# Softmax rows transposed on TensorE: probabilities, identity and output bank typed float32r instead of float32

## What is computed

```python
q, k, v = jnp.einsum('bsx,xMnd->Mbnsd', x, qkv)              # 16 heads of 64
a = jnp.einsum('bnsd,bntd->bnst', q, k) * q.shape[-1] ** (-0.5)
cum = jnp.cumsum(rpe_bias[:, :s], axis=-1)
rel = jnp.arange(s)[:, None] - jnp.arange(s)[None, :]
bias = jnp.where(rel >= 0, cum[:, jnp.clip(rel, 0)], PAD)    # PAD = -30000: causal
a = jax.nn.softmax(a + bias, axis=-1)
mix = jnp.einsum('bnst,bntd->bnsd', a, v)
attn = jnp.einsum('bnsd,ndx->bsx', mix, out_w)
x = layernorm(x + attn)
x = layernorm(x + ffn(x))    # ffn: sigmoid(xr W_r) * (relu(xk W_k)^2 W_v), xr and xk mixed with the token before
```

## Time and profile before

| | |
|---|---|
| median of 3 runs | 1161.54 us (1153.31 to 1162.71) |
| the profiled execution, its own time | 1157.7 us |
| its span, first to last instruction | 1156.0 us |
| PE busy | 1106.1 us, 96% |
| PE weight loads busy | 791.9 us, 69% |
| DVE busy | 809.3 us, 70% |
| ACT busy | 731.1 us, 63% |
| POOL busy | 6.4 us, 1% |
| DMA, share of 16 engines on the queue of SP | 62.1% |
| granted TensorE clock, mean | 0.99 of full speed |

### The profile page before, as it was taken

How to read it: one execution, slowest core, us unless ns; L and a number is a source line. 1 busy time by engine, 2 the same in 40 slices (tenths; PEclk the granted TensorE clock), 3 DMA queues, 4 the chain that set the end, 5 groups by cost and what they waited for, 6 DMA issues and landing times.

```text
span 1156.0 us, 21563 instructions
## 1 busy us (share of the span) xinstructions
PE 1106.1 (96%) x6973; PEld 791.9 (69%) x6973; DVE 809.3 (70%) x2121; ACT 731.1 (63%) x1857; POOL 6.4 (1%) x15
## 2 busy tenths in 40 slices
PE   6899999999999999999999999999999999999994
PEld 3666666766677777676777676777666777767773
DVE  2666666666657777776778777778776778777756
ACT  3666667665656676675766676767666667667633
POOL 1000000000000000000000000000000000000000
PEclk9999999999999999999999999999999999999998
DMA  8856565675657666656577656676756666665710
GB/s 200 222 142 150 140 153 145 152 186 137 155 135 168 160 166 161 169 144 174 134 176 171 166 149 155 163 177 164 185 135 155 164 169 158 169 164 144 234 40 20
DMA packets 113005, 180.71 MB, mean 156 GB/s; under 512 B 13152, under 2 KB 69360, under 8 KB 112896
## 3 DMA queue, kind: packets, MB, share of 16 engines
q1 hardware_dynamic: 110736, 178.42, 62.1%
q10 hardware_dynamic: 2160, 0.92, 0.3%
HBM read 58.41 MB, written 20.22 MB: 68 GB/s over the span
## 4 chain that ended last, share of the span: by engine, by line
PE 84%; DVE 5%; DMA 4%; issue 3%; ACT 2%; SPq 2%; POOL 0%; DVEq 0%; ACTq 0%
PE ps_o L1018 22%; PE ps_rows L977 21%; PE ps_t L994 17%; PE ps_m L952 9%; PE ps_m L957 5%; PE ps_m L1034 4%; PE ps_o L994 3%; DMA stacks<-k_lo 2%; DVE pt L684 2%; PE ps_rows L1090 1%; SPq L300 1%; DVE prob L660 1%; DMA prob<-in_L_attn_x 1%; ACT pt L519 1%; DVE mix_sb L691 1%
## 5 line engine op out<-in xcount | busy, mean ns | idle before, releaser
L501 ACT ACTIVATE prob<-prob,low 128x128 f32<-128x128 f32 (+7 forms) x512 | 394.5, 772 | 111.9 <-DVE low L660 106.0
L660 DVE CUSTOM_DVE_ANT_0 prob<-ps_rows,table 128x128 f32<-128x128 f32 (+7 forms) x512 | 379.9, 750 | 52.8 <-PE ps_rows L977 33.9
L977 PE MATMUL ps_rows<-stacks 128*128 128x512 f32 (+3 forms) x1536 | 401.1, 372 | 10.7 <-DMA stacks<-k_lo 6.1
L994 PE MATMUL ps_t<-ident,prob 128*128 128x128 f32 x1984 | 311.4, 278 | 6.4 <-ACT pt L519 3.5
L994 PEld LDWEIGHTS ps_t<-ident,prob 128*128 128x128 f32 x1984 | 231.4, 141 | 90.3 <-issue 74.6
L1018 PE MATMUL ps_o<-pt,v_pair 128*64 128x512 f32 (+3 forms) x1536 | 270.1, 494 | 0.0
L977 PEld LDWEIGHTS ps_rows<-stacks 128*128 128x128 f32 x1536 | 246.1, 190 | 32.0 <-DMA stacks<-k_lo 7.0
L684 DVE COPY pt<-ps_t 128x256 f32<-128x256 f32 (+2 forms) x320 | 178.2, 565 | 124.8 <-PE ps_t L994 124.2
L1018 PEld LDWEIGHTS ps_o<-pt,v_pair 128*64 128x64 f32 x1536 | 102.2, 137 | 177.5 <-issue 165.2
L519 ACT ACTIVATE pt<-ps_t 128x512 f32<-128x512 f32 (+3 forms) x352 | 162.8, 463 | 95.9 <-PE ps_t L994 95.6
L952 PE MATMUL ps_m<-x_cur,w_cur 128*128 128x512 f32 x250 | 131.6, 608 | 5.2 <-DVE q_lo L646 2.0
(11 more groups left out here) (118 smaller groups left out, 607.2 us busy)
## 6 DMA issues: line engine op xcount, KB each, us to landing
stacks<-k_hi SPq DMA_DIRECT2D x126, 256.0 KB, 4.6
stacks<-k_lo SPq DMA_DIRECT2D x126, 256.0 KB, 5.1
inv_all<-inverse_sums SPq DMA_DIRECT2D x128, 128.0 KB, 3.3
stacks<-q_hi SPq DMA_DIRECT2D x63, 256.0 KB, 4.0
stacks<-q_lo SPq DMA_DIRECT2D x63, 256.0 KB, 4.3
mix_transposed<-mix_sb SPq DMA_DIRECT2D x62, 256.0 KB, 3.8
table<-bias_by_distance SPq DMA_DIRECT2D x64, 192.0 KB, 3.6
mix_tile<-mix_transposed SPq DMA_DIRECT2D x24, 512.0 KB, 4.7
```

Source lines behind the costliest of these rows:

```text
L501: nc.scalar.activation(row, row, ACT.Exp, bias=low[:, r:r + 1], scale=-1.0, accum_out=total[:, r:r + 1]).then_inc(s_exp, 1)
L660: nc.vector.tensor_tensor_reduce(prob[:, r % PSLOTS, 0:width], ps_rows[:, score_at(r):score_at(r) + width], table[n % 2][:, h, 0:width][:, ...
L977: ins = nc.tensor.matmul(ps_rows[:, at + c0:at + c1], q_st(h, n)[:, P * i:P * i + P], k_st(h, n, low_part)[:, c0:c1], start=(low_part == 0 ...
L994: ins = nc.tensor.transpose(t_bank[TBANK[k]][:, P * b:P * b + P], prob[:, r % PSLOTS, at:at + P], ident[:, :])
```

## The change

The tiles `prob` and `ident` get a second name with type fp32r, and the 2304 transposes of probabilities (L994) read and write by the new types: data `prob_r`, identity `ident_r`, and the bank viewed as fp32r. `prob_r` lies on the same bytes as `prob` (it is allocated first and given back, and `prob` takes its place); DVE and ACT still write `prob` as f32, and the evacuations still read the banks as f32. `ident_r` is a tile of its own: POOL copies `ident` into it once, and PE waits for that copy ahead of its first instruction. The other transposes (`inv`, `x1`, x, the weights) stay f32. No other instruction changes, nor does the order of PE, DVE, ACT or SP.

```diff
+        with nc.sbuf_tensor("prob_r", [P, PSLOTS, SEQ], F32R) as prob_r:
+            pass
+        prob = sb("prob", [P, PSLOTS, SEQ])
         ident = sb("ident", [P, P])
+        ident_r = sb("ident_r", [P, P], F32R)
...
-        prob = sb("prob", [P, PSLOTS, SEQ])
...
+        s_identr = sem("identr")
...
             pool.affine_select(out=ident[:, :], in_=ident[:, :], compare_op=ALU.not_equal, fill=1.0, base=0,
                                pattern=[[-1, P]], channel_multiplier=1).then_inc(s_const, 1)
+            pool.wait_ge(s_const, 2)
+            nc.gpsimd.tensor_copy(ident_r[:, :], ident[:, :]).then_inc(s_identr, 1)
...
         def _(pe):
             pe.wait_ge(s_const, 2)
+            pe.wait_ge(s_identr, 1)
...
-                        ins = nc.tensor.transpose(t_bank[TBANK[k]][:, P * b:P * b + P], prob[:, r % PSLOTS, at:at + P],
-                                                  ident[:, :])
+                        ins = nc.tensor.transpose(t_bank[TBANK[k]][:, P * b:P * b + P].bitcast(F32R),
+                                                  prob_r[:, r % PSLOTS, at:at + P], ident_r[:, :])
```

## The result

The changed kernel takes 1129.81 us (median of 4 runs, 1128.80 to 1134.16) against 1158.34 (4 runs, 1153.31 to 1162.71): ratio 0.9766, 95% interval 0.974 to 0.9791. The forecast was 1100 us, 58 less than before. The profiled execution took 1129.46 us, and its span is 1127.7, 28.3 less than the 1156.0 before.

What follows compares the result with a forecast made beforehand. PE's own instructions were taken to set the pace; 1.82 us saved in each of 32 steps, 58 us off 1157.7, gave 1099.5, predicted as 1100. Likeliest range 1068 to 1115 (0.53); 1068 to 1164 holds 0.83.

Steps and rivals of the forecast that it cites:

- What bounds the kernel: One step's chain: PE's own instructions set the pace, PE leaving it only once, about a microsecond, for DVE to empty `ps_o`.
- The copy on POOL: Start of the kernel: POOL's copy of `ident` and PE's wait for it cost 0; without cover 0.6 us at most.
- The saving per transpose: Transposes of probabilities on PE: 75 ns each in fp32r against 109 in f32, saving 34 ns.
- rival of no change: An fp32r transpose still costs about 109 ns through weight load or double streaming; 1158 to 1162 us; load mean 190; chance 0.17.
- How much reaches the step: A step's 72 transposes: 0.8 us from 42 beside DVE's closed work, 1.02 from the other 30, 1.82 in all.
- DVE's block: Stretch 719.98 to 734.30 of a step, 42 transposes: DVE's work is closed from a bias to the copy of `ps_o`.
- The cap: Where DVE is nearly full, faster PE can only close DVE's gaps of 0.76 us; 0.8 counted in place of 1.43.
- The sum: Whole kernel: 1157.7 less 58 us (32 x 1.82) gives 1099.5; predicted 1100.
- What is late next: Next step's first score waits for head 0's `k_lo`; its DMA lands 1.2 us early and stays covered.
- Slower: With 128 columns an fp32r instruction falls back to 222 ns, 113 ns more per transpose; about 1418 us; chance 0.11.
- Large gain: A transpose at 56 ns: 1081 us with DVE's limit in force, 1036 without; chance 0.06 for under 1068.
- Small gain: Transposes shorten, but PE also meets ACT's evacuations in the 734.3 to 738.2 stretch; about 1131 us, 1115 to 1150; chance 0.13.

Runs made afterwards that it cites:

- The tail: The changed kernel with sequences of f32 and fp32r transposes and products added behind PE's last work; alone, an f32 transpose took 109 ns, an fp32r one 85 ns.

## Why the prediction was wrong, point by point

**What bounds the kernel: mostly right.** PE's own instructions set the pace in the rest of the step, and what they saved there arrived whole (0.58 to 0.60 us). But I took the one place where the chain leaves PE for PE's only wait, and that was wrong. The chain hides short waits, because a run's time in it holds what PE waited inside the run.

**The copy on POOL: right.** Cost 0, ratio 1.0005.

**The saving per transpose: wrong in size.** I took 34 ns for each of 72. Measured: 109 - 85 = 24 ns, and nothing for the first of each run, of which a step has 16. That is 56 x 24 ns = 1.34 us a step in place of 2.45, or 19 ns a transpose. The step that failed is the choice of 75 ns on the argument that the transpose's own load is the short one. The tail shows the f32 load in 62 ns (with 64 rows) and the fp32r one in 85. The line through the fp32r products (64 ns) was no lower bound either, since it knows only the stream. The Trainium skill's sustained 81 ns for a weight load and matmul pair of 128 columns ("TensorE: Matmul & The Clock Gate", on the back-to-back issue gap) was nearer than my 75: this case shows 85. (By the 81 ns my sum would have been 52.5 us and not below 52.) The rival of no change had the right mechanism, the load, and the wrong size. Its 107 ns for a product's load stood on no row of the kernel before; the tail shows 108 to 112. And its sign, the load's mean duration, told nothing: it stayed at 141 ns while the load set the pace.

**How much reaches the step: right in kind, wrong in size.** I split the step at the right places and said that DVE's block caps its part whatever a transpose costs. The cap was set at 0.8 us by adding up DVE's gaps. 0.36 came. Of the gaps, 0.27 stands unchanged in the changed kernel ahead of the bias at 702.05, where the bias waits for a score that PE issues ahead of the block's first transposes, and 0.17 of the 0.39 is left. Here, DVE's timeline in the changed kernel:

```profile
702.05 1.09 DVE L667 CUSTOM_DVE_ANT_0 prob<-ps_rows,table 128x896 f32<-128x896 f32 x1 [0.27 <-PE ps_rows L985]
...
714.31 0.69 DVE L691 COPY pt<-ps_t 128x512 f32<-128x512 f32 x1 [0.17 <-PE ps_t L1002]
```

And the first 3.60 us of the block have a fixed length that no transpose enters: score, bias on DVE, exponential and copy on ACT, bank 9. The 11 transposes between were among the 42 that I priced at 34 ns and capped together, and they saved nothing. So the second step that failed is the cap: a sum of gaps gave 0.8, and a path through DVE and ACT allowed 0.36.

**The sum.** With the measured rest and the measured block it is 0.58 + 0.36 = 0.94 for a late ordinary step, and 0.73 for an early one. Between the first step and the last, the first eight gave 9.0 us and the others 16.9; 1.7 came from an earlier first step that other executions do not share, and 0.7 from the end. That is 28.3. The forecast's 58 is 32 x 1.82, with the steps at the changes of a batch counted as all others.

**What is late next.** The DMA of `k_lo` did not become late in an ordinary step: it is not in the chain of the one shown. At the changes of a batch it is late before and after, and I had left it out there: PE waits 12.1 us for it in all with the change and 6.1 before.

**The rivals.** Slower: ruled out by the tail, 108 ns for an fp32r product of 128 columns, and 85 for the transpose. Large gain: ruled out by the same 85 ns, where it needed 56. Small gain: the time (1130) fell where this rival put it (1131), by another road. It took the loss in the stretch behind the block, on ACT, at a price of 34 ns; the loss was in the price and inside the block. That it came out at the measured time is luck.

## What to carry to other kernels

A shorter instruction pays only down to what it was hiding: here the weight load of its own next neighbour (85 ns) and that of the product behind each run, so count runs and not instructions. Before a price is extrapolated from rows of another kind, measure it alone; thirty-two of a kind behind the last output cost one run and give the 85 ns. Where a second engine is nearly full, do not add up its gaps: follow one dependence through it (score, bias, exponential, copy, next bank), since a path of fixed length caps the stretch earlier than the engine's busy time does.

## What the runs showed of the hardware that was not expected

The profile's duration of a weight load is no guide to its pace. Its mean is 140 to 141 ns for the loads of f32 transposes, which started as close as 62 ns apart (with 64 rows), and 141 for those of fp32r transposes, whose load alone kept them 85 ns apart.

In the tail's last sequence TensorE's granted clock fell while PE was busy all the time, in a run of 32 fp32r transposes with a stream of 64 columns and 64 rows of weights. The windows (us, PE, PEld, DVE, ACT, POOL, clock, DMA share, GB/s) show it:

```profile
1198.00:1199.50 1.50, 1.50 (x20) 1.50 (x19) 0.00 (x0) 0.00 (x0) 0.00 (x0) 1.00 0.00 0
1199.50:1201.30 1.80, 1.80 (x17) 1.74 (x16) 0.00 (x0) 0.00 (x0) 0.00 (x0) 0.57 0.00 0
```

It went from 2.4 to 1.2 GHz (0.57 is the mean of a window that begins just ahead of the fall). Ahead of it came 2.2 us of the same transposes in f32 and 1.5 us in fp32r. The spacing rose from 85 to 127 ns, by half and not to double. In the four sequences of 32 transposes with a stream of 128 columns the clock stayed at full speed. Which property of these transposes brought it down was not tried.
